# Attention and two expert layers on one core: the third and fourth score maxima moved ahead of the self products and of the result stages on VectorE, TensorE's small matmuls moved behind the fourth scores

## The reference, cut to what matters

```
query = seq2 + b_self                       # 16 items, 128 tokens, 16 heads of width 8
key   = [seq1 + b_prev, seq2 + b_self]
q, k, v = query @ Wq + bq, key @ Wk + bk, value @ Wv + bv
score_prev = q . k[first 128] * SCALE       # 128 x 128 for each head, masked by the item's length
score_self = (q * k[own token]).sum(-1)     # one for each token and head
weights = softmax([score_prev, score_self])
attn = weights[:-1] @ v[first 128] + weights[-1] * v[own token]
out  = attn @ Wo + bo                       # then gate logits, the two best experts, rows sent to them
```

## Time and profile before

| what | value |
|---|---|
| median of the runs | 517.86 us (511.44, 518.4, 517.86) |
| the profiled execution's own time | 516.34 us |
| its span, from first to last instruction | 514.6 us |
| TensorE matmuls busy | 433.5 us (84%), 2768 |
| VectorE busy | 290.3 us (56%), 1209 |
| ScalarE busy | 243.9 us (47%), 751 |
| GpSimd busy | 226.3 us (44%), 260 |
| mean granted TensorE clock | 0.925 |
| the attention's scores | from 19.0 us (first block) to 194 us (last) |

### The profile page before, as it was taken

How to read it: one execution, slowest core, us unless ns; L and a number is a source line. 1 busy time by engine, 2 the same in 40 slices (tenths; PEclk the granted TensorE clock), 3 DMA queues, 4 the chain that set the end, 5 groups by cost and what they waited for, 6 DMA issues and landing times.

```text
span 514.6 us, 11629 instructions
## 1 busy us (share of the span) xinstructions
PE 433.5 (84%) x2768; PEld 295.8 (57%) x2769; DVE 290.3 (56%) x1209; ACT 243.9 (47%) x751; POOL 226.3 (44%) x260
## 2 busy tenths in 40 slices
PE   3699989999999997799999999887582899898840
PEld 2355546565555644399898987356531467676630
DVE  2568898778878888423333332255362436576534
ACT  1277757777777774155454553245230123343310
POOL 3347783344333343524444443545566003555540
PEclk9999999999999998879999999878577799999985
DMA  2007999888889999656666660401111201222207
GB/s 60 10 13 178 255 244 244 215 229 216 222 213 246 242 237 314 190 167 178 174 172 178 173 180 22 163 0 37 38 47 47 52 1 37 67 77 70 62 16 242
DMA packets 58373, 71.10 MB, mean 138 GB/s; under 512 B 8754, under 2 KB 34599, under 8 KB 58208
## 3 DMA queue, kind: packets, MB, share of 16 engines
q1 hardware_dynamic: 52752, 60.89, 45.1%
q0 software_dynamic: 4736, 8.47, 5.1%
q10 hardware_dynamic: 848, 1.32, 0.9%
HBM read 35.58 MB, written 36.37 MB: 140 GB/s over the span
## 4 chain that ended last, share of the span: by engine, by line
PE 59%; DVE 15%; issue 8%; DMA 5%; ACT 5%; another core or an unknown queue 3%; POOL 3%; SPq 2%; ACTq 1%; POOLq 0%; DVEq 0%
PE bank L915 9%; PE bank L909 8%; PE bank L768 7%; PE bank L1079 5%; PE bank L780 5%; DVE mx L1413 3%; PE bank L1095 2%; PE bank L793 2%; DVE ps L1420 2%; PE bank L1005 2%; PE bank L1006 2%; PE bank L1016 2%; PE bank L1094 2%; ACT ps L1131 1%
## 5 line engine op out<-in xcount | busy, mean ns | idle before, releaser
L1226 ACT ACTIVATE hT<-bank,w 128x128 f32<-128x128 f32 x176 | 51.0, 368 | 56.0 <-PE bank L909 40.0
L768 PE MATMUL bank<-qexp 128*128 128x512 f32 x128 | 70.7, 635 | 0.8 <-POOL qexp L677 0.8
L698 POOL DMA_INDIRECT expert_outputs<-yb,idr x44 | 43.2, 983 | 57.8 <-DVE yb L1586 40.7
L686 POOL DMA_INDIRECT expert_rows<-rows,slots x32 | 31.5, 986 | 83.7 <-DVE slots L1436 76.6
L748 POOL DMA_INDIRECT layer_outputs<-w_all,idr x40 | 39.3, 983 | 63.5 <-DVE w_all L1785 48.3
L780 PEld LDWEIGHTS bank<-ident,ps 128*128 128x128 f32 x256 | 33.0, 142 | 54.0 <-ACT ps L1137 26.0
L1137 ACT ACTIVATE ps<-bank,ntop 128x128 f32<-128x128 f32 x192 | 54.8, 378 | 7.6 <-DVE ntop L1416 7.6
L780 PE MATMUL bank<-ident,ps 128*128 128x128 f32 x256 | 48.8, 295 | 5.7 <-ACT ps L1131 2.7
L915 PE MATMUL bank<-w_all,hT 128*128 x352 | 50.3, 287 | 2.5 <-ACT hT L1226 1.6
L1146 ACT ACTIVATE pT<-bank 128x512 f32<-128x512 f32 x64 | 38.2, 597 | 28.7 <-PE bank L780 26.5
L1413 DVE TENSOR_REDUCE mx<-bank 128x4 f32<-128x512 f32 x64 | 44.0, 687 | 13.7 <-PE bank L768 8.7
(11 more groups left out here) (294 smaller groups left out, 897.9 us busy)
## 6 DMA issues: line engine op xcount, KB each, us to landing
expert_rows<-fill SPq DMA_DIRECT2D x64, 390.0 KB, 6.0
w<-in_L_ffn_w_dram SPq DMA_DIRECT2D x40, 258.0 KB
w_all<-in_L_ffn_w_dram SPq DMA_DIRECT2D x24, 256.0 KB
xt<-expert_rows SPq DMA_DIRECT2D x45, 65.0 KB
w_all<-expert_rows SPq DMA_DIRECT2D x40, 65.0 KB, 1.2
qexp<-layer_outputs SPq DMA_DIRECT2D x4, 512.0 KB, 5.7
aux<-in_L_ffn_b_dram SPq DMA_DIRECT2D x1, 1536.0 KB
qexp<-expert_outputs SPq DMA_DIRECT2D x3, 512.0 KB, 3.8
```

The source lines that it names most:

```text
L698: g.indirect_dma_start(ys_dram, bass.IndirectOffsetOnAxis(ap=idr[r][:, 0:1], axis=0), yb[r][:, :], None, bounds_check=YS1 - 1, oob_is_err= ...
L768: pe.matmul(psA[j % 2][:, :], qexp[p][:, j, :], kexp[p].rearrange("p g k -> p (g k)"), start=True, stop=True).then_inc(a_in_ps, 1)
L1226: s.activation(hT[r % 2][:, c, :], banks[c][:, 0:P], ACT.Gelu, bias=w1[r][:, F0 + c:F0 + c + 1]).then_inc(gelu_done, 1)
```

## The change

The change moves three things. No instruction is added or taken away on any engine. On VectorE the maxima of set 2 move from behind prod to ahead of it, and the maxima of set 3 from behind att to directly behind prod, ahead of the wait for the middle matmuls. On TensorE the fourth scores move ahead of the middle matmuls and of their wait for prod. A wait for VectorE's own chain (cm.join) is put ahead of mm, since the maxima no longer stand directly before it.

```
 TensorE, step:
                 scores(i, p, 2)
                 turned_weights(i, 1, 2)
                 weighted_values(i, p, 0, 2)
+                scores(i, p, 3)
                 if active(i, 1):
                     pe.wait_ge(prod_ready, i)
                 ...
                     m = pe.matmul(ps_self, prod[:, :], ind[:, :], start=True, stop=True)
                 if m is not None:
                     m.then_inc(mid_in_ps, 1)
-                scores(i, p, 3)
                 turned_weights(i, 2, 2)
                 weighted_values(i, p, 1, 2)
 VectorE, step:
                                            op0=ALU.subtract, op1=ALU.mult).then_inc(kA_ready, 1)
+                below_maximum(i, p, 2)
+                if active(i, 1):
                     cq.join()
                     dve.wait_ge(qb_ready, i)
                     atleast(dve, mid_in_ps, i - 1)
                     v.scalar_tensor_tensor(out=prod[:, :], in0=ps_ks, scalar=cself[:, 0:1], in1=qb[:, :],
                                            op0=ALU.add, op1=ALU.mult).then_inc(prod_ready, 1)
-                below_maximum(i, p, 2)
+                below_maximum(i, p, 3)
                 ...
-                below_maximum(i, p, 3)
                 if active(i, 2):
+                    cm.join()
                     cm.link(v.scalar_tensor_tensor(out=mm[:, :], in0=mx[:, :], scalar=nolen[:, bass.ds(i - 2, 1)], in1=nself[p][:, :],
```

## The result

The changed kernel took 519.63 us (median of 18 runs, 516.17 to 522.7) against 516.91 us of the kernel before, run beside it (18 runs). The ratio is 1.0068 with a 95% interval of 1.0046 to 1.0091: slower by about 3.5 us (the ratio is that of the means, 519.6 and 516.3; the medians are 2.7 apart), clear of noise, though within 2%. I had forecast 515.4 us, a little faster. The sign was wrong. That the number lay in the range says little, since the range had been widened by the spread of the runs and by the rivals. The span of the profiled execution rose from 514.6 to 518.6 us.

A forecast was written before the change was run, and what follows sets the result against it. TensorE was taken to bound the attention. Terms of 0 for eight middle steps, -0.7 (step 6), -0.6 (steps 2 and 3) and +0.4 (step 17) gave -0.9 us on 516.34: 515.4 us, range 509 to 523.5.

The forecast's parts named there:

- The middle steps: Steps 8 to 15: ntop of set 2 still ends with GpSimd's first expansion; net 0, between 0 and +0.1 us a step.
- The seam: Where GpSimd's first expansion meets its second: ntop gets in unless the expansion starts right behind a send; gaps stay unchanged.
- The odd steps: Steps outside the middle: in step 6 ntop arrives ahead of the expansion, -0.7 us; steps 2, 3, 16 and 17 priced separately.
- I take -0.6: Steps 2 and 3 together: maxima 2 move up more, ntop comes to the expansions' seam; -0.6 of a possible 0 to -1.5 us.
- the sum: Whole attention: 0 for eight middle steps, -0.7, -0.6 and +0.4, together -0.9 us.
- meets the second expansion as before: Steps 4 and 5: ntop is held by GpSimd's second expansion as in the kernel before; no term in the total.
- Step 17: Last step, no prod: maxima 3 now stand between the fourth scores and rank; +0.4 us, between 0 and +0.85.
- ntop is free: Rival: ntop is not held by GpSimd, so set 2's exponentials start earlier; 510 us, chance 0.08.
- VectorE becomes the bound: Rival: VectorE's 0.50 us of slack behind sm is used up; +3.6 us over 12 steps, 519 us, chance 0.14.
- ntop misses the seam: Rival: in eight steps ntop ends with the second expansion, 1.0 us later; 523 us, 531 with clock lost, chance 0.20.
- The step 6 stall goes whole: Rival: step 6's ntop stall vanishes with its clock loss; -3.8 us in place of -0.7, 512 us, chance 0.12.

The follow-up runs named there:

- a3: New order only in steps 8 and later, old order in steps 0 to 7, against the kernel before: 486.49 us, ratio 0.999.
- a4: New order only in steps 0 to 7, old order from step 8 on, against the kernel before: 490.36 us, ratio 1.006.
- h1: Changed kernel with two GpSimd fills between the two sends of steps 9, 11 and 13, so the expansion starts right behind a send: 491.88 us, one run.
- g1: Changed kernel with GpSimd's constants cut small and spread, plus a short fill and wait ahead of the expansion in steps 6, 7 and 16: 483.49 us, one run.
- a2: Changed kernel with GpSimd's twenty pooling-constant operations moved behind the attention: 496.11 us, ratio 1.016 against the kernel before.
- a1: Kernel before (old order) with GpSimd's twenty pooling-constant operations moved behind the attention: 501.51 us, ratio 1.0268 against the kernel before.
- k1: g1 with the old order in step 17: 482.53 us, ratio 0.9925 against the kernel before.

## Why the prediction was wrong

**The middle steps: right.** Net 0 with a range to +0.1 a step was forecast; 0.21 for eight was measured, and 0.0 between a3 and a4. ntop's end with the first expansion and the new wait for prod showed. In steps 8 to 11 sm ended 0.25 to 0.32 later, as forecast, and the idle time behind it, 0.36 to 0.51 us before, was 0.11 to 0.40. That the transposes of set 2 would no longer be held was wrong, without a price.

**The seam: right in its cause, wrong in its reach.** That GpSimd's start behind a send decides, and not the arrival, was my reading of two cases; h1 and g1 show it. But I took it as fixed which steps start so ("kA's time and so the gap stay"). Step 7 changed sides: the second send ended 0.42 behind kA (85.78 to 85.36) where it had ended 0.21 ahead of it, and the seam was missed for 0.7 us. The kernel before was the exception. In step 7 kA ended 4.37 or 4.38 us behind the end of set 0's ntop in the changed kernel and in all experiments but a3 and a4, and 4.90 before, 5.00 in a3, 4.58 in a4. These three are the kernels in which the stretch at granted clock 0.50 reached into step 7: to 78.56 before, with the step's start at 78.20. In the changed kernel it was over at 79.22, with the start at 80.82. By this reading TensorE's low clock had made kA late and so kept ntop free. No run tested it by itself.

**The odd steps: wrong, and the step that failed.** "Without prod ahead, mx starts about 0.25 earlier and ntop arrives at about 69.5, ahead of the expansion" gave -0.7. In the trace mx of set 2 stands idle for 0.29 us until the third scores end at 71.32; ntop came at 72.09, 0.17 behind the expansion's start, and took 2.89, so of the stall of 3.01 only 0.12 went. The held ntop of set 0 did not cause this: in a2, where it took 0.17, mx has the same 0.29 of idle time and ntop comes 0.14 behind the start of the expansion. What the prediction took as fixed and was not is the start of the expansion. Before, rank (L1431) of step 6 was held for 0.55 us to the end of an L661 (65.43), and slots, the sends and the expansion behind it: the expansion started 5.42 us behind the end of set 0's ntop. In the changed kernel rank took 0.17 and the expansion started 5.06 behind, while the third scores kept their 4.46. Step 6 lost 1.03 where I had a gain; 0.98 of it is the hold of set 0's ntop (1.15 for 0.17).

"I take -0.6" for steps 2 and 3 was +0.62, of which the 0.39 of step 2 is within what that step varies by. Its ntop came 0.01 behind the start of the second expansion (1.04 long). In step 3 it did slip in (0.17), but mm behind it was then held for 1.31. With the constants out of the way step 3 gave the forecast gain: 10.28 in a1, 9.56 in a2.

**What the sum left out** was the larger error: I followed the two ntop and forgot that in steps 3 to 6 each two-input operation behind them, att, mm and sm, moves too, and meets another of GpSimd's constants. For steps 4 and 5 I wrote that ntop "meets the second expansion as before", and it did. But mm, held 1.30 instead of never, pushed sm and the next step's ntop by 0.2 us, from 0.05 ahead of L661 to 0.14 behind it. That is 1.1 in step 5 and 1.0 in step 6. By steps, the way from the forecast -0.9 to the measured +3.9 (3.67 and 0.28 behind the last ntop) is 1.7 in step 6, 1.2 in steps 2 and 3, 1.1 in step 5, 0.7 in step 7 and 0.2 in the middle.

**Step 17**: +0.4 was forecast; 0.3 was measured between the kernels and 0.5 between g1 and k1.

The rivals: *ntop is free* is refuted by every held ntop. *VectorE becomes the bound* did not occur: some idle time was left behind sm in every middle step looked at. *ntop misses the seam* occurred in one step more than before, step 7, and not by its arrival. *The step 6 stall goes whole* needed the constants spread and the pause ahead of the expansion (g1).

## What to carry to other kernels

List every operation of VectorE with two inputs in SBUF and every GpSimd operation that reads SBUF, and lay them against each other for each step, with the margin by which they miss each other; an order that moves one of them by a quarter microsecond moves all behind it. Where margins are 0.05 to 0.1 us, as here, do not price the middle of a loop alone: the few steps with other work on GpSimd held nearly all of the loss. Look also at what a stall in the kernel before may happen to protect, as the one in step 6 seems to have done with the seam of step 7. And where GpSimd has background work, cut it small and put it where VectorE reads PSUM: in the attention that was worth 2.5 us for the old order and 6.9 for the new, where the new order by itself is worth 0.8. Only part of it was seen in the time.

## What the runs showed of the hardware that I had not expected

- A VectorE operation that waits for GpSimd gets in between two GpSimd operations that follow each other without a gap, if the first of them had started 0.08 us or more behind the end of what GpSimd did ahead of it. Over all thirteen traces, of ntop of set 2 arriving during the first expansion, this was so 107 times out of 107. It does not get in if that one started 0.02 to 0.03 us behind an indirect DMA of GpSimd: 33 times out of 33 (step 6, steps 7 and 16, and the three steps of h1), whether it arrived 0.04 or 0.68 us into the expansion. The one case at 0.05 (step 7 of a4) got in. One fill of 128x1 with a wait on it, 0.2 us, changes the one into the other. The prediction's reading, that the cores of GpSimd run out of step behind a send, is shown by no run.
- scalar_tensor_tensor with two inputs in SBUF (mm) is held like tensor_tensor: 1.30 us instead of 0.23. The Trainium skill ("SBUF — State Buffer", Who interferes with whom) speaks of any VectorE instruction with two SBUF inputs, and the trace agrees.
